# Sixteen-head cross attention on one core: the probabilities of a half-tile step turned and applied in five pieces of 124 instead of twice three of 103

## The chip, the core and the metric

The kernel is one program on one NeuronCore of a Trainium2 chip. The metric is device time in microseconds (us), the median of several executions. The engines named here are TensorE (PE in the rows, with its weight loads as PEld), VectorE (DVE), ScalarE (ACT), GpSimd (POOL) and SyncE (SP), which only issues DMAs.

## The reference, cut to what matters

Four blocks follow each other on x of shape (4, 512, 128). Each is a cross attention and an FFN with several experts. The change touches the first three attentions only, which have 16 heads of width 8 and attend to 77 context rows per batch:

```python
q = split_heads(queries @ Wq + bq)          # b, 16 heads, 512, 8
k = split_heads(keys @ Wk + bk)             # b, 16 heads,  77, 8
v = split_heads(values @ Wv + bv)
scores = jnp.einsum('bhqd,bhkd->bhqk', q, k) / jnp.sqrt(jnp.float32(HD))
scores = jnp.where(mask, jnp.float32(-1e15), scores)
attn = jax.nn.softmax(scores, axis=-1)
ctx = jnp.einsum('bhqk,bhkd->bhqd', attn, v)
x = x + ctx_as_rows @ Wo + bo               # no Wo in the second attention
```

The second and third are alike up to masks and biases. The fourth attention has 8 heads of width 128 and code of its own.

## The kernel before

x has 2048 rows, held as 16 tiles of 128 query rows on the partitions. An attention `l` (0, 1, 2) walks over 32 steps `n`, two to a tile, `t = n // 2`. A step handles 8 of the 16 heads for one tile, as two groups of 4 heads. A group has 4 x 77 = 308 scores per row, so a step has 616. I call a step without any other work in it a plain step.

TensorE runs iteration `n` in this order, written out by hand: `scores(n)` (two matmuls per group, one with the queries and one that adds the mask), the two `turn`s of step n-2, on odd n `turn_out` (the finished tile is transposed), the two `values` of step n-3, on even n `project` (times Wo), and what the plan `APLAN` adds in that iteration. The additions are `q` (the next batch's queries), `v` (`spread_values`, the next batch's value matrix), `x` (transposes of a finished batch for the FFN), and in the first and third attention `l` and `c` (routing). `turn_out` and `project` do not exist in the second attention.

A `turn(k)` transposes one group's 308 probabilities, padded to 309, in three pieces of 103 (line L1925), into PSUM bank 4 or 5. ScalarE copies them to one of four buffers `pT` (L1007, 103 x 384). `values(k)` multiplies the three pieces with three slices of `vx` and accumulates them in a window of 126 columns of bank 6 (L1938). Each fp32 matmul of L1938 shows as two rows in the trace, so a step has 12. `vx` is a value matrix with zeros wherever the head of a row is not the head of a column. It is built for each batch by `spread_values` (L1894, three matmuls, six rows in the trace) and by VectorE's `values_low` (L1409), which multiplies with the mask `cmask`.

VectorE does `shift(n)`: the row maximum of each head (L1422) and the subtraction (L1425). ScalarE follows with the exponential (L1001). VectorE also divides by the sums (`norm`, L1432 and L1437, on odd n), adds to x (L1450), takes statistics (L1456, L1459), and makes the low parts of q (L1273, L1276) and x (L1250).

Scores, `q`, `v`, `x`, `l` and `c` share a ring of two pairs of PSUM banks. An item waits until the item two places ahead of it has been read: scores(n) waits for `shift(n-2)` in a plain stretch, and for VectorE's `values_low` or low part of q if a `v` or `q` stands in that place.

The constants `cmask`, `spread` and the ones in `vx` are made once by GpSimd at the start (L686 to L715). The semaphore `consts` releases TensorE and VectorE after them.

Of the kernel before, what the change touches and what calls it, by code (L numbers as in the profile page):

```python
# [4 lines left out]
B, S, D = 4, 512, 128  # L5
KC = 77
P = 128
# [9 lines left out]
NCH = 3  # L17
CH = -(-GW // NCH)
GWP = NCH * CH
VC = HD + 1  # L20
VW, VSTEP = 126, 6
OSTEP = 128 + HG * VC - VSTEP
# [26 lines left out]
def build(nc, x_in, ctx_t, ctx_rows, mask0, mask1, mask2, attn_w, cols, rows, gates,  # L49
# [8 lines left out]
    with stack:  # L58
# [31 lines left out]
        def ycols(b):  # L90
# [29 lines left out]
        cmask = sb("cmask", [CH, NCH, NG, HG])  # L120
        spreadp = sb("spreadp", [KC, GWP])
        spread = spreadp[:, 0:GW].rearrange("k (h c) -> k h c", h=HG)
# [12 lines left out]
        probs = [shared[:, 2 * NG * GW + s * NG * GWP:2 * NG * GW + (s + 1) * NG * GWP]  # L135
                 .rearrange("p (g k) -> p g k", g=NG) for s in range(2)]
        act_out = [sb(f"act_out{s}", [P, 512]) for s in range(2)]
        pT = [sb(f"pT{s}", [CH, NCH * P])[:, :] for s in range(2)] + [act_out[s][0:CH, 0:NCH * P] for s in range(2)]
# [537 lines left out]
        def _(pool):  # L676
# [26 lines left out]

            for j in range(NCH):
                g.affine_select(out=cmask[:, j], in_=cmask[:, j], compare_op=ALU.is_ge, fill=0.0,
                                base=CH * j, pattern=[[0, NG], [-KC, HG]], channel_multiplier=1)
            st.link(g.affine_select(out=spread, in_=spread, compare_op=ALU.not_equal, fill=1.0, base=0,
                                    pattern=[[0, HG], [-1, KC]], channel_multiplier=1))
            for j in range(NCH):
                g.affine_select(out=cmask[:, j], in_=cmask[:, j], compare_op=ALU.is_ge, fill=0.0,  # L710
                                base=KC - 1 - CH * j, pattern=[[0, NG], [KC, HG]], channel_multiplier=-1)
# [208 lines left out]
        def _(act):  # L920
# [72 lines left out]
            def attention(l):  # L993
                f, lo = FFNS[l], (0 if l == 0 else 1)

                def softmax(n):
                    act.wait_ge(s_used, NSTEP * l + n + 1)
                    if n >= 4:
                        act.wait_ge(pt_ready, 2 * (NSTEP * l + n - 3))
                    t, g = n // 2, slice(2 * (n % 2), 2 * (n % 2) + 2)  # L1000
                    a.activation(probs[t % 2][:, g, 0:GW], shifted[t % 2][:, g, :], ACT.Exp).then_inc(p_ready, 1)  # L1001
# [236 lines left out]
        def _(dve):  # L1238
# [163 lines left out]
            def attention(l):  # L1402
                f, lo = FFNS[l], (0 if l == 0 else 1)

                def values_low(b, o):
                    dve.wait_ge(vx_ps, B * l + b + 1)
                    if b >= 2:
                        dve.wait_ge(pv_done, 2 * NSTEP * l + 16 * (b - 1))
                    v.tensor_tensor(  # L1409
                        vx[b % 2][:, :, :, 0:HD].rearrange("r j h d -> r (j h) d"),  # L1410
                        bank(o)[0:CH, 0:NCH * D].rearrange("r (n d) -> r n d", d=HD),
                        bcast(cmask[:].rearrange("r j g h -> r (j g h)"), HD, 2),
                        ALU.mult).then_inc(vx_ready, 1)
# [14 lines left out]
                def norm(t):  # L1428
                    dve.wait_ge(pv_done, 2 * NSTEP * l + 4 * t + 4)
                    o4 = psum[:, 6 * 512:6 * 512 + NG * OSTEP].rearrange("p (g c) -> p g c", g=NG)[:, :, 0:HG * VC  # L1430
                        ].rearrange("p g (h c) -> p g h c", h=HG)
                    st.link(v.reciprocal(rden[:].rearrange("p (g h) -> p g h", g=NG), o4[:, :, :, HD]))  # L1432
# [4 lines left out]
                    v.tensor_tensor(onorm[t % 2][:].rearrange("p (g h) d -> p g h d", g=NG), o4[:, :, :, 0:HD],  # L1437
                                    bcast(rden[:].rearrange("p (g h) -> p g h", g=NG), HD, 3), ALU.mult
                                    ).then_inc(o_used, 1)
# [30 lines left out]
                for s in range(2):  # L1470
                    st.link(v.memset(probs[s][:, :, GW:GWP], 0.0))
# [284 lines left out]
        def _(pe):  # L1756
# [110 lines left out]
            def attention(l):  # L1867
# [46 lines left out]
                def turn(k):  # L1914
                    n, t, g = k // 2, k // 4, k % 4
# [8 lines left out]
                    for j in range(NCH):  # L1924
                        ins = nc.tensor.transpose(bank(4 + k % 2)[0:CH, j * P:(j + 1) * P],  # L1925
# [3 lines left out]
                def values(k):  # L1929
                    t, g, b = k // 4, k % 4, k // 16  # L1930
                    if k % 16 == 0:
                        pe.wait_ge(vx_ready, B * l + b + 1)
                    if g == 0 and t:
# [3 lines left out]
                    for j in range(NCH):  # L1937
                        ins = mm(bank(6)[:, g * P:g * P + VW], pT[k % 4][:, j * P:(j + 1) * P],  # L1938
# [393 lines left out]
```

## Time and profile before

| | us |
|---|---|
| three runs | 1611.57, 1616.33, 1621.27 |
| median | 1616.33 |
| the profiled execution | 1614.35 |
| its span in the trace | 1612.6 |
| TensorE busy in the span | 1405.3 (87%) |
| VectorE busy | 1096.3 (68%) |
| ScalarE busy | 957.3 (59%) |
| mean granted TensorE clock | 0.951 of full speed |

The three changed attentions lie at about 43 to 160 us, 277 to 380 us and 653 to 764 us of the span. The rest is the four FFNs and the fourth attention. Rows are read like this: start, duration, engine, line, operation, output <- input, partitions x elements. Rows of one kind that follow each other are merged, with their count. In brackets stand the idle time before the row and what ended it.

### The profile page before, as it was taken

The numbers are of one execution on the slowest core, as the hardware profiler recorded it, in microseconds if no ns is written. First come the engines' busy times: TensorE is split into PE (matmuls) and PEld (weight loads), VectorE is DVE, ScalarE is ACT, GpSimd is POOL, SyncE is SP. The second block draws the span as 40 slices with busy tenths as digits, with TensorE's granted clock in tenths as the row PEclk, the third lists the DMA queues.
The fourth block names the chain that finished last, engine by engine and source line by source line (L and its number), as shares of the span: only waits on it lengthen the run. The fifth ranks groups of instructions, "written<-read, shape, count | busy, mean of one in ns | idle before, by whom it ended". The sixth has DMA issues, their size and how long they took to land. (4 is left out here: it accounts for less than half of the span.)

```text
span 1612.6 us, 24666 instructions
## 1 busy us (share of the span) xinstructions
PE 1405.3 (87%) x8205; PEld 1203.9 (75%) x8205; DVE 1096.3 (68%) x2253; ACT 957.3 (59%) x1895; POOL 517.6 (32%) x860
## 2 busy tenths in 40 slices
PE   5799898999999999899899996998898988727773
PEld 5699575898888888798688875887786877527773
DVE  3676689786666667776577775776776766536664
ACT  3456776565555555556777775665565665426661
POOL 5324522303112111422321112222434424355673
PEclk7899999999999999999999998899999999859997
DMA  6111141110000010121121000920000000034542
GB/s 160 54 39 40 45 160 61 40 60 1 4 37 21 20 40 7 35 69 52 40 79 66 26 1 16 190 31 1 6 10 1 14 1 6 9 119 154 158 155 88
DMA packets 57533, 85.22 MB, mean 53 GB/s; under 512 B 9400, under 2 KB 39536, under 8 KB 56127
## 3 DMA queue, kind: packets, MB, share of 16 engines
q1 hardware_dynamic: 54911, 79.40, 18.1%
q0 software_dynamic: 2496, 4.24, 0.8%
q8 instruction: 67, 1.10, 0.3%
q14 instruction: 59, 0.48, 0.1%
HBM read 57.90 MB, written 15.78 MB: 46 GB/s over the span
## 5 line engine op out<-in xcount | busy, mean ns | idle before, releaser
L1553 DVE TENSOR_TENSOR hhl<-psum,hhl 128x512 fp32r<-128x512 f32 x336 | 230.2, 686 | 94.6 <-ACT hhl L1074 92.8
L1760 PE MATMUL psum<-xh,wl 128*128 128x512 f32 (+1 forms) x520 | 203.9, 392 | 7.7 <-DVE logits L1285 4.2
L1761 PE MATMUL psum<-xl,wh 128*128 128x512 f32 (+1 forms) x528 | 202.6, 384 | 0.0
L1762 PE MATMUL psum<-xh,wh 128*128 128x512 f32 (+1 forms) x528 | 202.2, 383 | 0.0
L1074 ACT ACTIVATE hhl<-psum 128x512 fp32r<-128x512 f32 x336 | 199.4, 594 | 0.7 <-DVE psum L1549 0.7
L1146 ACT ACTIVATE hhl<-psum 128x512 fp32r<-128x512 f32 (+1 forms) x160 | 95.3, 596 | 136.9 <-PE psum L2157 136.5
L884 POOL TENSOR_SCALAR shared<-shared,xrd 128x589 f32<-128x589 f32 x128 | 97.7, 765 | 231.4 <-DVE xrd L1647 230.7
L1064 ACT ACTIVATE psum<-psum 128x512 f32<-128x512 f32 x208 | 121.2, 583 | 74.4 <-PE psum L1762 73.3
L1062 ACT ACTIVATE act_out<-psum 128x512 f32<-128x512 f32 x128 | 76.4, 598 | 119.7 <-PE psum L1762 119.3
L1549 DVE TENSOR_TENSOR psum<-act_out,psum 128x512 f32<-128x512 f32 x128 | 88.9, 695 | 84.2 <-PE psum L1762 75.7
L1652 DVE TENSOR_TENSOR hhl<-psum,hhl 128x512 fp32r<-128x512 f32 (+1 forms) x160 | 110.2, 689 | 52.1 <-ACT hhl L1146 51.8
L2060 PE MATMUL psum<-hhl,wl 128*128 128x512 f32 x336 | 135.7, 404 | 10.6 <-DVE hhl L1553 8.7
L2061 PE MATMUL psum<-hhl,wh 128*128 128x512 f32 x336 | 133.0, 396 | 0.0
L2062 PE MATMUL psum<-hhl,wh 128*128 128x512 f32 x336 | 132.4, 394 | 0.0
L801 POOL TENSOR_SCALAR wh<-wraw 128x512 fp32r<-128x512 f32 (+1 forms) x42 | 29.5, 703 | 290.1 <-PE psum L2062 279.9
L1760 PEld LDWEIGHTS psum<-xh,wl 128*128 128x128 f32 x520 | 98.4, 189 | 28.5 <-DVE logits L1285 4.9
L1762 PEld LDWEIGHTS psum<-xh,wh 128*128 128x128 f32 x528 | 100.9, 191 | 21.2
L1761 PEld LDWEIGHTS psum<-xl,wh 128*128 128x128 f32 x528 | 100.7, 191 | 19.0
L1641 DVE TENSOR_REDUCE xnm<-psum 128x1 f32<-128x589 f32 x128 | 97.5, 762 | 21.6 <-PE psum L1762 20.7
L2157 PE MATMUL psum<-ident,shared 128*128 128x128 f32 (+1 forms) x640 | 98.4, 277 | 13.4 <-POOL shared L884 13.3
L1138 ACT ACTIVATE shared<-psum,xnm 128x589 f32<-128x589 f32 x128 | 96.0, 750 | 15.3 <-DVE xnm L1641 14.1
L1422 DVE TENSOR_REDUCE smax<-psum 128x8 f32<-128x616 f32 x96 | 76.2, 794 | 38.3 <-PE psum L1910 38.1
(370 smaller groups left out, 3725.7 us busy)
## 6 DMA issues: line engine op xcount, KB each, us to landing
shared<-in_f_dram SPq DMA_DIRECT2D x16, 768.0 KB
shared<-comb_dram SPq DMA_DIRECT2D x10, 1024.0 KB
xs_dram<-wraw SPq DMA_DIRECT2D x2, 4615.0 KB
shared<-comb_dram SPq DMA_DIRECT2D x24, 256.0 KB, 5.4
wraw<-in_f_dram SPq DMA_DIRECT2D x8, 768.0 KB
xn<-in_f_dram SPq DMA_DIRECT2D x7, 768.0 KB
wraw<-in_f_dram SPq DMA_DIRECT2D x9, 512.0 KB
hhl<-qh SPq DMA_DIRECT2D x64, 64.0 KB, 2.0
```

Of the source, the lines that this page charges most:

```text
L884: g.tensor_scalar(xprob[m % XS], xprob[m % XS], xrd[:, z], 1.0, ALU.mult, ALU.mult).then_inc(x_norm, 1)
L1064: ins = a.activation(h_bank(f, k), h_bank(f, k), f.func)
L1074: a.activation(hh[k % 4], h_bank(f, k), ACT.Copy).then_inc(f.hh_done, 1)
L1553: v.tensor_tensor(hl[k % 4], h_bank(f, k), hh[k % 4].bitcast(f32), ALU.subtract).then_inc(f.h_ready, 1)
L1652: v.tensor_tensor(hl[k % 4][r, :], bank(5 + k % 2)[r, :], hh[k % 4][r, :].bitcast(f32), ALU.subtract).then_inc(xt_lo, 1)
L1760: mm(dst, ll, rh, start=start, stop=False)
L1761: mm(dst, lh, rl, start=False, stop=False)
L1762: return mm(dst, lh, rh, start=False, stop=stop)
L2060: mm(dst, lo[:, o:o + P], hh[k % 4], start=(c == 0), stop=False)
L2061: mm(dst, hi[:, o:o + P], hl[k % 4], start=False, stop=False)
L2062: mm(dst, hi[:, o:o + P], hh[k % 4], start=False, stop=(c == f.nf - 1)).then_inc(f.h_used, 1)
L2157: ins = nc.tensor.transpose(bank(5 + k % 2)[r, qt * P:(qt + 1) * P], xprob[(4 * u + qt) % XS][:, j * P:j * P + r.stop], ident[:])
```

## The change

The two groups of 4 heads of a step become one row of 8 heads with 616 probabilities, padded to 620, in five pieces of 124. The first `turn`, ScalarE copy and `values` of a step take three of the pieces (`PARTS[0]`), the second take two. All five accumulate in one window of 126 columns. `vx` now has five slices instead of three, and `cmask`, `spread` and `spread_values` grow with it. The value matrix of a batch has 5 x 128 = 640 columns in PSUM instead of 384 and lies across two banks of its pair. Two of the four `pT` buffers move into the weight array `aw`, and the exponential writes one contiguous row of 616.

```diff
-NCH = 3
-CH = -(-GW // NCH)
-GWP = NCH * CH
+PH = 2 * HG
+PW = PH * KC
+NCH = 5
+CH = -(-PW // NCH)
+PWP = NCH * CH
+PARTS = (range(0, 3), range(3, NCH))
...
-VW, VSTEP = 126, 6
-OSTEP = 128 + HG * VC - VSTEP
+VW, VSTEP = 126, 18
+OSTEP = 128 + PH * VC - VSTEP
...
-        cmask = sb("cmask", [CH, NCH, NG, HG])
-        spreadp = sb("spreadp", [KC, GWP])
+        cmask = sb("cmask", [CH, NCH, 2, PH])
+        spreadp = sb("spreadp", [KC, PWP])
...
-        pT = [sb(f"pT{s}", [CH, NCH * P])[:, :] for s in range(2)] + [act_out[s][0:CH, 0:NCH * P] for s in range(2)]
+        pT = [aw[0:CH, 4 * P + 3 * P * s:4 * P + 3 * P * (s + 1)] for s in range(2)] + [
+            act_out[s][0:CH, 0:3 * P] for s in range(2)]
...
-                    a.activation(pT[k % 4], bank(4 + k % 2, NCH * P)[0:CH, :], ACT.Copy).then_inc(pt_done, 1)
+                    w = len(PARTS[k % 2]) * P
+                    a.activation(pT[k % 4][:, 0:w], bank(4 + k % 2, w)[0:CH, :], ACT.Copy).then_inc(pt_done, 1)
...
-                        bank(o)[0:CH, 0:NCH * D].rearrange("r (n d) -> r n d", d=HD),
+                        psum[0:CH, o * 512:o * 512 + NCH * D].rearrange("r (n d) -> r n d", d=HD),
...
-                        ins = mm(bank(o)[0:CH, j * D:(j + 1) * D], spreadp[:, j * CH:(j + 1) * CH],
+                        ins = mm(psum[0:CH, o * 512 + j * D:o * 512 + (j + 1) * D], spreadp[:, j * CH:(j + 1) * CH],
...
-                    for j in range(NCH):
-                        ins = nc.tensor.transpose(bank(4 + k % 2)[0:CH, j * P:(j + 1) * P],
+                    for i, j in enumerate(PARTS[k % 2]):
+                        ins = nc.tensor.transpose(bank(4 + k % 2)[0:CH, i * P:(i + 1) * P],
                                                   probs[t % 2][:, g, j * CH:(j + 1) * CH], ident[:])
...
-                    for j in range(NCH):
-                        ins = mm(bank(6)[:, g * P:g * P + VW], pT[k % 4][:, j * P:(j + 1) * P],
+                    for i, j in enumerate(PARTS[k % 2]):
+                        ins = mm(bank(6)[:, g * P:g * P + VW], pT[k % 4][:, i * P:(i + 1) * P],
```

TensorE's instructions of iteration 3 of the first attention (the one with a `spread_values`) before, as the program lists them. L1908 and L1910 are the scores, L1925 the turns, L1938 the values, L1894 the spreading and L1775 an `x` item:

```order
L1908 MATMUL psum<-kb,hhl 128x308
L1910 MATMUL psum<-maskneg,identb 128x308
L1908 MATMUL psum<-kb,hhl 128x308
L1910 MATMUL psum<-maskneg,identb 128x308
L1925 MATMUL psum<-ident,shared 103x128 x6
L1938 MATMUL psum<-vx0,pT0 128x126 x3
L1938 MATMUL psum<-vx0,pT1 128x126 x3
L1894 MATMUL psum<-vrows,spreadp 103x128 x3
L1775 MATMUL psum<-ident,xn 128x128 x4
```

The same iteration now, with line numbers 8 higher:

```order
L1916 MATMUL psum<-kb,hhl 128x308
L1918 MATMUL psum<-maskneg,identb 128x308
L1916 MATMUL psum<-kb,hhl 128x308
L1918 MATMUL psum<-maskneg,identb 128x308
L1933 MATMUL psum<-ident,shared 124x128 x5
L1946 MATMUL psum<-vx0,aw 128x126 x5
L1902 MATMUL psum<-vrows,spreadp 124x128 x5
L1783 MATMUL psum<-ident,xn 128x128 x4
```

Nothing changes its place. The turns and the values have one instruction less each, the spreading has two more.

VectorE at the end of its iteration 4 of the first attention before (the step's maximum and subtraction, then the value matrix, then work on the gate weights):

```order
L1250 TENSOR_TENSOR xl<-psum,xh 128x512
L1422 TENSOR_REDUCE smax<-psum 128x8
L1425 TENSOR_TENSOR shared<-psum,smax 128x616
L1409 TENSOR_TENSOR vx<-psum,cmask 103x48x8
L1535 TENSOR_SCALAR gwg<-gw,pcols 128x8
```

And now:

```order
L1258 TENSOR_TENSOR xl<-psum,xh 128x512
L1430 TENSOR_REDUCE smax<-psum 128x8
L1433 TENSOR_TENSOR shared<-psum,smax 128x616
L1417 TENSOR_TENSOR vx<-psum,cmask 124x80x8
L1543 TENSOR_SCALAR gwg<-gw,pcols 128x8
```

The place is the same, and the value matrix has 80 x 8 elements per row instead of 48 x 8.

## Rows read from the trace of the kernel before

**Rows 1.** The page: its span.

```profile
span 1612.6 us, 24666 instructions
```

**Rows 2.** Busy time by stretch: TensorE, weight loads, VectorE, ScalarE, GpSimd, clock, DMA.

```profile
120.00:140.00 20.00, 20.00 (x173) 18.94 (x173) 15.44 (x38) 13.17 (x30) 7.37 (x26) 1.00 0.17 51
300.00:320.00 20.00, 19.42 (x161) 17.81 (x160) 16.41 (x38) 11.03 (x22) 2.61 (x10) 1.00 0.13 31
353.00:368.00 15.00, 15.00 (x130) 14.12 (x129) 13.40 (x32) 9.79 (x19) 2.60 (x10) 1.00 0.01 1
```

**Rows 3.** Timeline, a plain step of the second attention on TensorE.

```profile
305.85 0.39 PE L1908 MATMUL psum<-kb,hhl 96*128 96x308 f32 x1
...
306.53 0.82 PE L1925 MATMUL psum<-ident,shared 128*103 128x128 f32 x6
...
307.18 1.50 PE L1938 MATMUL psum<-vx,pT 103*128 103x126 f32 x12
...
308.44 0.47 PE L1760 MATMUL psum<-xh,wql 128*128 128x512 f32 x1
```

**Rows 4.** Timeline, four transposes of full width and what follows them.

```profile
329.07 0.60 PE L1775 MATMUL psum<-ident,xn 128*128 128x128 f32 x4
329.43 0.39 PE L1908 MATMUL psum<-kb,k 96*128 96x308 f32 x1
```

**Rows 5.** Timeline, one `spread_values` and the item behind it.

```profile
290.85 0.82 PE L1894 MATMUL psum<-vrows,spreadp 77*103 77x128 f32 x6
291.50 0.60 PE L1775 MATMUL psum<-ident,xn 128*128 128x128 f32 x4
```

**Rows 6.** Groups by line and form over the span: count, busy us, mean ns, idle before.

```profile
L1409 DVE TENSOR_TENSOR vx<-psum,cmask 103x384 f32<-103x384 f32 x12 | 6.6, 549 | 1.4 <-PE psum L1894 1.3
...
L1425 DVE TENSOR_TENSOR shared<-psum,smax 128x616 f32<-128x616 f32 x96 | 76.7, 799 | 3.3
```

**Rows 7.** Timeline, iterations 10 and 12 of the second attention: what releases the next scores.

```profile
309.22 0.30 PE L1908 MATMUL psum<-kb,hhl 96*128 96x308 f32 x1
...
311.56 0.74 DVE L1273 SCALAR_TENSOR_TENSOR ql<-psum,pcols,qh 128x512 fp32r<-128x512 f32 x1
...
312.35 0.41 PE L1908 MATMUL psum<-kb,hhl 96*128 96x308 f32 x1 [0.39 <-DVE ql L1273]
...
315.61 0.39 PE L1908 MATMUL psum<-kb,hhl 96*128 96x308 f32 x1
...
318.04 0.55 DVE L1409 TENSOR_TENSOR vx<-psum,cmask 103x384 f32<-103x384 f32 x1
...
318.64 0.41 PE L1908 MATMUL psum<-kb,hhl 96*128 96x308 f32 x1 [0.19 <-DVE vx L1409]
```

**Rows 8.** Timeline, VectorE over one tile of the second attention (two plain steps).

```profile
300.98 0.26 DVE L1432 RECIPROCAL rden<-psum 128x16 f32<-128x16 f32 x1 [0.36 <-PE psum L1938]
...
304.14 0.80 DVE L1422 TENSOR_REDUCE smax<-psum 128x8 f32<-128x616 f32 x1 [0.25 <-PE psum L1910]
...
306.13 0.26 DVE L1432 RECIPROCAL rden<-psum 128x16 f32<-128x16 f32 x1 [0.36 <-PE psum L1938]
```

**Rows 9.** Timeline, first attention, from the stall at 64 us to the one at 77.

```profile
64.56 0.30 PE L1946 MATMUL psum<-ident,onorm 128*128 128x128 f32 x1 [2.37 <-DVE onorm L1437]
...
64.69 2.64 PE L1938 MATMUL psum<-vx,pT 103*128 103x126 f32 x12
...
70.65 0.47 PE L1997 MATMUL psum<-ident,wraw 77*128 77x77 f32 x4
...
71.58 0.51 SPq L569 DMA_DIRECT2D hhl<-qh  x1
```

**Rows 10.** Timeline, the start: GpSimd's last constant and VectorE's first instruction.

```profile
6.62 0.43 POOL L715 COPY vx<-cmask 103x48 f32<-103x48 f32 x2
...
8.17 0.54 DVE L1369 TENSOR_SCALAR wraw<-psum,pcols 128x308 f32<-128x308 f32 x1 [8.17 <-DMA bo<-in_rows_dram]
...
12.10 0.87 DVE L1354 BATCH_NORM_STATS2 stats<-x 128x6 f32<-128x128 f32 x4 [1.57 <-DMA x<-in_x_dram]
```

More of the change, by code:

```diff
@@ L119, in build @@
         hm32 = sb("hm32", [KS, HG])
-        cmask = sb("cmask", [CH, NCH, NG, HG])
-        spreadp = sb("spreadp", [KC, GWP])
-        spread = spreadp[:, 0:GW].rearrange("k (h c) -> k h c", h=HG)
+        cmask = sb("cmask", [CH, NCH, 2, PH])
+        spreadp = sb("spreadp", [KC, PWP])
+        spread = spreadp[:, 0:PW].rearrange("k (h c) -> k h c", h=PH)
         kb = sb("kb", [P, 10 * S], f32r)
@@ L134, in build @@
                    for s in range(2)]
-        probs = [shared[:, 2 * NG * GW + s * NG * GWP:2 * NG * GW + (s + 1) * NG * GWP]
-                 .rearrange("p (g k) -> p g k", g=NG) for s in range(2)]
+        probs = [shared[:, 2 * NG * GW + s * 2 * PWP:2 * NG * GW + (s + 1) * 2 * PWP]
+                 .rearrange("p (g k) -> p g k", g=2) for s in range(2)]
         act_out = [sb(f"act_out{s}", [P, 512]) for s in range(2)]
-        pT = [sb(f"pT{s}", [CH, NCH * P])[:, :] for s in range(2)] + [act_out[s][0:CH, 0:NCH * P] for s in range(2)]
+        pT = [aw[0:CH, 4 * P + 3 * P * s:4 * P + 3 * P * (s + 1)] for s in range(2)] + [
+            act_out[s][0:CH, 0:3 * P] for s in range(2)]
         oT = [act_out[s][:, 384:512] for s in range(2)]
@@ L999, in softmax @@
                         act.wait_ge(pt_ready, 2 * (NSTEP * l + n - 3))
-                    t, g = n // 2, slice(2 * (n % 2), 2 * (n % 2) + 2)
-                    a.activation(probs[t % 2][:, g, 0:GW], shifted[t % 2][:, g, :], ACT.Exp).then_inc(p_ready, 1)
+                    t, g = n // 2, n % 2
+                    a.activation(probs[t % 2][:, g, 0:PW],
+                                 shifted[t % 2][:, 2 * g:2 * g + 2, :].rearrange("p g k -> p (g k)"),
+                                 ACT.Exp).then_inc(p_ready, 1)
                 def copy_pT(k):
@@ L1429, in norm @@
                     dve.wait_ge(pv_done, 2 * NSTEP * l + 4 * t + 4)
-                    o4 = psum[:, 6 * 512:6 * 512 + NG * OSTEP].rearrange("p (g c) -> p g c", g=NG)[:, :, 0:HG * VC
-                        ].rearrange("p g (h c) -> p g h c", h=HG)
-                    st.link(v.reciprocal(rden[:].rearrange("p (g h) -> p g h", g=NG), o4[:, :, :, HD]))
+                    o4 = psum[:, 6 * 512:6 * 512 + 2 * OSTEP].rearrange("p (g c) -> p g c", g=2)[:, :, 0:PH * VC
+                        ].rearrange("p g (h c) -> p g h c", h=PH)
+                    st.link(v.reciprocal(rden[:].rearrange("p (g h) -> p g h", g=2), o4[:, :, :, HD]))
                     if l == 1:
@@ L1914, in turn @@
                 def turn(k):
-                    n, t, g = k // 2, k // 4, k % 4
+                    n, t, g = k // 2, k // 4, k // 2 % 2
                     if k % 2 == 0:
@@ L1929, in values @@
                 def values(k):
-                    t, g, b = k // 4, k % 4, k // 16
+                    t, g, b = k // 4, k // 2 % 2, k // 16
                     if k % 16 == 0:
                         pe.wait_ge(vx_ready, B * l + b + 1)
-                    if g == 0 and t:
+                    if k % 4 == 0 and t:
                         pe.wait_ge(o_used, NT * l + t)
```

12 lines of the change are left out of this document (6 added, 6 removed).

## The prediction, made before the changed kernel was run

> **What bounds the kernel now.** I first read the page for the span and the clock, then the busy time by stretch inside the three attentions, then the timeline of single steps on TensorE and VectorE. The changed code runs in about 330 of the 1612.6 us [rows 1]. There TensorE is the bound: 20.00 of 20 us busy at 120 to 140, 19.42 at 300 to 320, 15.00 of 15 at 353 to 368, all at a granted clock of 1.00 (2.4 GHz) [rows 2]. VectorE comes second: 13.40 of those last 15 us. ScalarE has room with 9.79. So an instruction taken from TensorE is worth its time only until VectorE's chain is met, and the question is how often that happens.
>
> **The removed work.** A plain step of the second attention takes 308.44 - 305.85 = 2.59 us [rows 3]: 0.68 for scores, 0.65 for the six turns (0.108 each), 1.26 for the twelve value rows (0.105 each). The change takes away one turn and one value matmul, which is two rows: 0.108 + 0.210 = 0.318 us per step, 96 steps, 30.5 us at most. The pieces are larger, 124 instead of 103. For a transpose that is a wider weight tile. Transposes of 128 columns follow each other at (329.43 - 329.07) / 4 = 0.09 us [rows 4], no slower than those of 103, so I take the price per instruction as unchanged. For the values only the rows of the contraction grow, and I take the 126-column price as it is. The second ScalarE copy of a step shrinks from 384 to 256 columns; ScalarE is not waited for, so that is worth nothing.
>
> **The added work.** `spread_values` goes from three matmuls to five, six rows to ten. Six take 291.50 - 290.85 = 0.65 us [rows 5], so four more cost 0.43 us, twelve times: 5.2 us on TensorE. VectorE's value matrix goes from 384 to 640 elements. The nearest rows are 549 ns at 384 elements and 799 ns at 616, both fp32 products of PSUM and SBUF [rows 6]: 250 ns for 232 elements, so 640 elements come to about 0.82 us, +0.28. From below that could be +0 if the length did not count, from above 549 x 640 / 384 = 915 ns, +0.37. I take the slope of the two rows. GpSimd's constants at the start grow (four more selects, twice the width of `spread`), an estimate of 1 to 2 us. They end at 7.05 us, VectorE waits for a DMA until 8.17 and again 1.57 us for x before 12.10 [rows 10]; I cost it at nothing, and at up to 1 us if that cover is gone.
>
> **Where the removed time arrives.** I sort the iterations by what ends them.
>
> (a) TensorE is full, no item of the ring stands in the way. I count 18 such steps in the first attention, 23 in the second, 22 in the third: iterations 5 to 8 (not in the first attention), 9, 13 to 17 and 21 to 33, without 27 in the first and third. 63 x 0.318 = 20.0 us gained, and three last values outside, 0.6. Sum -20.7.
>
> (b) The iteration after a `q` is ended by VectorE's low part of q: scores at 309.22, low part done at 312.30, next scores at 312.35 [rows 7]. This chain begins at the scores and has nothing of the change in it. Iterations 10 and 18 everywhere, and 27 in the first and third attention, where routing stands in that place: eight steps, 0.
>
> (c) Iterations with a spreading (3, 11, 19). TensorE has 0.43 more and 0.32 less: +0.12, six times, 0.7. In three of them (3 in the first attention, 19 in the first and third) the spreading itself waits for VectorE, so only the +0.43 counts: 1.3. Sum +2.0.
>
> (d) The iteration after the spreading (4, 12, 20) is ended by the value matrix on VectorE: scores at 315.61, value matrix 318.04 + 0.55, next scores at 318.64 [rows 7]. It gets longer by 0.28, nine times, and once more at the start of the third attention, where VectorE is late: +2.8. Here the change costs directly what it was meant to save elsewhere.
>
> (e) The first attention's stretch from 64.5 to 71 us. SyncE's queue reloads wraw there and waits for the transposes of 70.65 that read it; the query DMAs of the next batch go out behind it at 71.58 and TensorE stands until they land [rows 9]. Between lie twelve value rows at half clock (2.64 us, about 0.20 a row), one turn block and one more value block at full clock. 0.40 + 0.11 + 0.21 = 0.7 us gained. Before 64.5 us VectorE is the bound, so the steps there gain nothing.
>
> (f) In the second attention both engines come to about the same length. From 300.98 to 306.13 VectorE has 5.15 us for two steps, of which it waits 0.25 and 0.36 [rows 8]; so it needs some 4.54. TensorE would need 2 x 2.27 = 4.54. A tie between two engines that wait for each other costs something: I put 0.035 us on each of 14 steps, +0.5.
>
> Sum: -20.7 + 2.0 + 2.8 - 0.7 + 0.5 = -16.1 us. From the profiled execution, 1612.6 of span and 1.75 around it, that gives 1598.2. That execution was 2.0 us under the median of the three runs; from the median it gives 1600.2. I forecast 1600.
>
> **A rule against it.** The trace shows transposes of 128 columns in 0.09 us each and of 103 in 0.108 [rows 3, 4], so width does not show in their spacing. The Trainium skill, "TensorE: Matmul & The Clock Gate", section "LDWEIGHTS (loading the stationary operand)", says that a weight load takes time in proportion to its columns and not to the rows of the contraction. By that rule, if loads set the pace, five wide turns would take as long as six narrow ones. The trace does not agree with it as the bound here; that result is the third rival.
>
> **The rivals.**
>
> 1. The full TensorE gain. VectorE's chains of (b) and (d) give way because VectorE is less pressed elsewhere. Then 30.5 - 5.2 = 25.3 us arrive: 1591. For it: VectorE is busy only 15.44 of 20 us in the first attention [rows 2]. Against it: those chains start at the scores, not at VectorE's backlog [rows 7]. 10%.
>
> 2. VectorE becomes the bound. Already 13.40 of 15 us in the second attention [rows 2]; with the larger value matrix, and TensorE no longer slower, the steps stop at VectorE's pace everywhere. Then about half of (a) arrives, 10.3 less: 1600.2 + 10.3 = 1610.5. Against it: in the first and third attention a plain step has a transpose and a projection more on TensorE and VectorE has several tenths free. 16%.
>
> 3. The turns cost by their width. Five at 0.108 x 124 / 103 = 0.130 take 0.65, as six do now. Then 63 x 0.108 = 6.8 us of (a) are lost: 1607. Against it: rows 4. 7%.
>
> 4. Slower than before, by the clock. TensorE is full now at 1.00 in these stretches. If it stands often enough for the granted clock to fall to 1.2 GHz there, a step costs much more: the value rows take 2.64 instead of 1.50 us [rows 3, 9], 1.14 more, and turns and scores about as much again, some 2.4 us a step as an estimate. Seven such steps undo the gain, ten more than that cost 24: with twelve in all the time is 1600 + 29 = 1629. For it: every attention now has more waits. Against it: 300 to 320 has 0.58 us of idle time and a clock of 1.00 [rows 2], and the new waits are tenths of a microsecond. 5%.
>
> **How the numbers follow.** My forecast 62%, the rivals 10, 16, 7 and 5. The chip's own spread, 1611.57 to 1621.27 in three runs, is as wide as half the effect, and where the clock dips in the later stages may shift with the start of the FFNs by a few microseconds either way. The range takes in rival 1 with 2 us below and rival 2: 1589 to 1611. Left out are rival 4 and the tails. 0.5% is 8 us, about what a measurement of this kernel can tell from no change: the bound is 1608.3. Faster: 0.62 x 0.96 + 0.10 + half of rival 3 and a fifth of rival 2, 0.77. Slower by over 0.5% is rival 4, 0.05. Same: 0.18.
>
> **What would show it.** The plain step of the second attention should fall from 2.59 to between 2.27 and 2.32 us, and that of the first and third, which is longer by a transpose or a projection, by 0.32. Turns and value rows keep 0.108 and 0.105 us apart. The value matrix takes 0.82 us, and the wait of scores for it grows. Iterations 12 and 20 get longer by 0.28, iteration 10 stays at 3.13. The FFNs and everything behind 766 us keep their lengths. I am wrong if plain steps fall by less than 0.25 (VectorE in front), if the turns' spacing rises (width), or if the clock inside an attention falls below 1.00 where it was 1.00 before.

## The result and the profile after

| | us |
|---|---|
| before, 19 runs | 1614.69 (1607.76 to 1621.27) |
| after, 19 runs | 1603.85 (1598.80 to 1610.52) |
| ratio | 0.9933, 95% interval 0.9920 to 0.9945 |
| profiled execution after, its span | 1601.09, 1599.4 |

The change takes 10.8 us off, an interval of 9 to 13. The forecast was 16.1. The profiled executions are 13.2 us apart in span, so about 2 of those are the spread between executions.

The page after, for [rows 1]: 476 instructions fewer on all engines together.

```profile
span 1599.4 us, 24190 instructions
```

Busy time by stretch (TensorE, weight loads, VectorE, ScalarE, GpSimd, clock, DMA), for [rows 2], and then the three attentions as windows from their first scores to the scores of their last step. First the kernel after:

```profile
300.00:320.00 20.00, 18.48 (x151) 16.81 (x150) 17.42 (x38) 11.94 (x26) 2.60 (x10) 1.00 0.17 41
43.58:145.69 102.11, 90.09 (x671) 80.83 (x670) 78.34 (x177) 53.48 (x121) 32.95 (x79) 0.92 0.16 43
272.64:358.04 85.40, 76.85 (x607) 68.86 (x606) 74.34 (x159) 53.58 (x112) 21.88 (x54) 0.98 0.17 47
643.25:737.28 94.03, 83.96 (x667) 75.97 (x665) 72.01 (x157) 56.43 (x128) 31.59 (x71) 0.98 0.15 43
```

The same three windows of the kernel before:

```profile
45.49:149.41 103.92, 93.97 (x744) 85.47 (x743) 78.33 (x179) 56.77 (x122) 33.47 (x80) 0.97 0.16 42
278.10:368.52 90.42, 85.70 (x679) 78.19 (x678) 73.52 (x158) 56.87 (x113) 21.60 (x53) 0.95 0.16 45
654.56:750.91 96.35, 91.12 (x739) 83.79 (x738) 71.67 (x158) 59.82 (x129) 32.12 (x74) 0.98 0.16 42
```

Over the three windows TensorE is busy 19.9 us less (270.8 to 250.9), but they last only 9.2 us less (290.7 to 281.5). The other 10.7 us are new idle time of TensorE. In the second attention it is 8.9 us less work and 5.0 us less time. VectorE works 1.2 us more (223.5 to 224.7).

A plain step of the second attention on TensorE, for [rows 3]:

```profile
296.54 0.39 PE L1916 MATMUL psum<-kb,hhl 96*128 96x308 f32 x1
...
297.22 0.71 PE L1933 MATMUL psum<-ident,shared 128*124 128x128 f32 x5
297.76 1.28 PE L1946 MATMUL psum<-vx,act_out 124*128 124x126 f32 x10
298.80 0.39 PE L1916 MATMUL psum<-kb,hhl 96*128 96x308 f32 x1
```

It takes 2.26 us: 0.68 for scores, 0.54 for five turns, 1.04 for ten value rows. Before it was 2.59.

Iterations 10 to 12 of the same attention, on TensorE and VectorE, for [rows 7]:

```profile
301.90 0.31 PE L1916 MATMUL psum<-kb,hhl 96*128 96x308 f32 x1
...
304.24 0.74 DVE L1281 SCALAR_TENSOR_TENSOR ql<-psum,pcols,qh 128x512 fp32r<-128x512 f32 x1
...
305.04 0.41 PE L1916 MATMUL psum<-kb,hhl 96*128 96x308 f32 x1 [0.72 <-DVE ql L1281]
...
307.39 1.26 PE L1902 MATMUL psum<-vrows,spreadp 77*124 77x128 f32 x10
308.40 0.38 PE L1916 MATMUL psum<-kb,hhl 96*128 96x308 f32 x1
...
310.82 0.81 DVE L1417 TENSOR_TENSOR vx<-psum,cmask 124x640 f32<-124x640 f32 x1
...
311.69 0.41 PE L1916 MATMUL psum<-kb,hhl 96*128 96x308 f32 x1 [0.80 <-DVE vx L1417]
```

Iteration 10 lasts 3.14 us as before, and the wait inside it has grown from 0.39 to 0.72: the 0.33 us taken from TensorE became a wait. Iteration 12 lasts 3.29 instead of 3.03, with a wait of 0.80 where there was 0.19.

### The profile page after: what moved, and what is told of

Same layout as the page of the kernel before. It is cut to its first block and busy times, and to the rows that moved or that the text cites. A ratio compares the mean times of both kernels' runs of the same rounds, so it can differ in the third digit from the quotient of the medians.

```text
span 1599.4 us, 24190 instructions
## 1 busy us (share of the span) xinstructions
PE 1381.8 (86%) x7965; PEld 1177.0 (74%) x7965; DVE 1098.4 (69%) x2253; ACT 947.2 (59%) x1895; POOL 519.3 (32%) x864
## 5 line engine op out<-in xcount | busy, mean ns | idle before, releaser
L2165 PE MATMUL psum<-ident,shared 128*128 128x128 f32 (+1 forms) x640 | 98.6, 277 | 13.3 <-POOL shared L889 13.2
```

What stands on the lines that cost most here:

```text
L2165: ins = nc.tensor.transpose(bank(5 + k % 2)[r, qt * P:(qt + 1) * P], xprob[(4 * u + qt) % XS][:, j * P:j * P + r.stop], ident[:])
```

## How the experiments are read

The time of a whole run moves by several us between executions of one program, which is most of what is to be told apart here. What lies outside the three windows is 1313 to 1324 us in all 14 profiles, whatever the edit. So I give for each run the median, the ratio to the kernel before on the same chip, and the windows. A window comes from one profiled execution.

The windows are not all equally steady. Two profiles of the kernel after agree within 0.1 us in each, but two profiles of one reordered kernel (e3_vq_first and e3_again) differ by 0.5, 0.9 and 0.8 us in the three, with both signs, and only their sums, 270.40 and 270.03, lie close together. The differences lie in iterations 0 to 9, where TensorE leaves waits of 1 to 4 us and the granted clock is at half in places. The last column holds iterations 10 to 30 of the three attentions alone. There the granted clock is 1.00 in every profile, and the two pairs of profiles agree within 0.05 us. It is the firmest number here.

| kernel | median | ratio (95%) | windows 1, 2, 3 | sum | iterations 10 to 30 |
|---|---|---|---|---|---|
| before | 1614.69 | 1 | 103.92, 90.42, 96.35 | 290.69 | 189.24 |
| after | 1603.85 | 0.9933 (0.9920 to 0.9945) | 102.11, 85.40, 94.03 | 281.54 | 180.47 |
| after_again | 1603.85 | 0.9929 (0.9908 to 0.9949) | 102.18, 85.35, 94.00 | 281.53 | 180.42 |
| e1_small_vx | 1599.74 | 0.9894 (0.9875 to 0.9913) | 99.00, 83.95, 92.21 | 275.16 | 176.34 |
| e7_before_big_vx | 1620.36 | 1.0034 (1.0018 to 1.0050) | 108.96, 92.51, 102.30 | 303.77 | 193.33 |
| e5_extra_turn | 1609.10 | 0.9961 (0.9946 to 0.9976) | 103.51, 88.36, 96.14 | 288.01 | 183.93 |
| e6_extra_value | 1618.73 | 1.0022 (1.0008 to 1.0037) | 107.02, 90.53, 98.72 | 296.27 | 189.38 |
| e2_v_first | 1597.45 | 0.9880 (0.9861 to 0.9900) | 100.76, 84.58, 92.27 | 277.61 | 175.61 |
| e3_vq_first | 1593.91 | 0.9854 (0.9832 to 0.9876) | 100.13, 81.30, 88.97 | 270.40 | 172.86 |
| e3_again | 1595.11 | 0.9869 (0.9843 to 0.9895) | 99.67, 82.21, 88.15 | 270.03 | 172.85 |
| e8_gate_later | 1586.40 | 0.9828 (0.9801 to 0.9856) | 93.28, 81.75, 88.99 | 264.02 | 172.78 |
| e9_logits_first | 1580.61 | 0.9788 (0.9758 to 0.9817) | 91.68, 81.60, 86.81 | 260.09 | 169.99 |
| e4_before_vq_first | 1608.19 | 0.9925 (0.9902 to 0.9948) | 105.07, 87.06, 92.92 | 285.05 | 185.13 |
| e10_before_all | 1597.04 | 0.9879 (0.9855 to 0.9902) | 97.30, 87.44, 93.99 | 278.73 | 183.62 |

The theory is that of the prediction: TensorE's steps get shorter by what is removed, except where VectorE's low part of q or its value matrix ends them, and the larger value matrix costs its full length there.

## Is the larger value matrix on the path? e1 and e7

e1 spreads and masks three slices of `vx` instead of five; it leaves out slices 3 and 4 of every value matrix, which stay zero.

```diff
-                    for j in range(NCH):
+                    for j in range(3):
                         ins = mm(psum[0:CH, o * 512
...
-                        vx[b % 2][:, :, :, 0:HD]
+                        vx[b % 2][:, 0:3, :, 0:HD]
```

> The changed kernel, but the value matrix is built as small as before: three spreading matmuls instead of five, and VectorE multiplies 384 columns instead of 640 (slices 3 and 4 keep zeros, so that part of the values is left out). Theory (the added work sits on the path): nine spreading steps lose 0.43 us on TensorE each, ten waits for the value matrix lose 0.28 us each, so 3.9 + 2.8 = 6.7 us less than the changed kernel: a ratio to before near 0.989. Rival (the added work is hidden beside other work and the missing gain lies elsewhere): no more than 2 us less, ratio 0.992 to 0.993.

The windows fall by 6.4 us, the ratio by 0.0039. VectorE's product on the path, in e1:

```profile
304.90 0.55 DVE L1419 TENSOR_TENSOR vx<-psum,cmask 124x384 f32<-124x384 f32 x1
...
305.50 0.41 PE L1918 MATMUL psum<-kb,hhl 96*128 96x308 f32 x1 [0.53 <-DVE vx L1419]
```

Iteration 11 of the second attention goes from 3.36 to 2.93 (0.43), iteration 12 from 3.29 to 3.02 (0.27), iteration 4 from 3.92 to 3.66 (0.26). Over all nine pairs of such iterations the spreading gives 3.9 us and the value matrix 2.3, and iterations 10 to 30, which hold six of the pairs, fall by 4.1. Both terms of the prediction arrive in full, with nothing hidden. That the windows' 6.4 is so near the 6.2 is in part chance: iteration 6 of the first attention is 1.3 us shorter as well, and iterations 0 to 2 of the second and third are 0.9 longer together.

e7 does the reverse on the kernel before: it spreads and masks 640 columns, of which 384 are used.

```diff
-                        bank(o)[0:CH, 0:NCH * D]
+                        psum[0:CH, o * 512:o * 512 + 5 * D]
...
-                    for j in range(NCH):
+                    for j in range(5):
+                        c = min(j, 2) * CH
```

> The kernel before with the larger value matrix alone: five spreading matmuls and 640 columns on VectorE, of which the values read three slices as before (two of the pT buffers lie in the weight array, as in the changed kernel, for want of room). Theory: 3.9 us on TensorE and 2.5 to 2.8 us of waits, 6.5 us slower than before, ratio 1.004. Rival (the longer value matrix costs only because TensorE got faster): 4 us, ratio 1.0025.

The medians give +5.3 us, between the two expectations. The second attention's window gives +2.1, which is 3 x (0.43 + 0.27). Iterations 10 to 30 give +4.1, which is 6 x (0.43 + 0.27). The first and third windows give +5.0 and +6.0, of which some 2 each lie at the changed items. The rest lies elsewhere: iteration 3 of the third attention lasts 7.93 instead of 3.69 us, iterations 6 and 8 of the first 5.06 and 5.33 instead of 3.93 and 4.10. These are places where TensorE comes out of a long wait (the granted clock is 0.50 from 668 to 680 us in e7), and the section on the prediction returns to them. The windows' sum of +13.1 is that of one execution, 4.4 us slower than e7's median, and it lies outside what the ratio allows (3 to 8 us).

## What is one turn worth, and one value matmul? e5 and e6

e5 adds to the kernel after one transpose per step, of a piece that is turned anyway, into columns that nobody reads.

```diff
+                    if k % 2:
+                        ins = nc.tensor.transpose(bank(4 + k % 2)[0:CH, 2 * P:3 * P],
+                                                  probs[t % 2][:, g, 4 * CH:5 * CH], ident[:])
                     ins.then_inc(pt_ready, 1)
```

> The changed kernel with a sixth transpose in each step (the last piece once more, into columns that nobody reads). Theory: only in the steps that TensorE fills does it cost, about 60 of 96 by 0.108 us: 6.5 us more than the changed kernel (10.4 if every step paid; 0 if VectorE were the bound). Rival (a turn of 124 columns is dearer than one of 103): 0.130 us each, 8 us or more, and the spacing of the turns in the trace is 0.13.

It is 5.2 us behind after_again by the medians, 6.5 by the windows and 3.5 in iterations 10 to 30. Its plain step, after five turns:

```profile
303.58 0.71 PE L1933 MATMUL psum<-ident,shared 128*124 128x128 f32 x5
304.12 0.27 PE L1936 MATMUL psum<-ident,shared 128*124 128x128 f32 x1
304.23 1.28 PE L1949 MATMUL psum<-vx,act_out 124*128 124x126 f32 x10
```

Five wide turns take 0.54 us and the sixth 0.11. They cost by the piece and not by their width. The rule of the Trainium skill ("TensorE: Matmul & The Clock Gate", section "LDWEIGHTS (loading the stationary operand)") that the time of a weight load goes by its columns does not set the pace here: loads of 124 columns and of 103 both leave transposes 0.108 us apart.

The windows' 6.5 equals the expectation by chance, since iteration 3 of the second attention is 1.7 us longer at a granted clock of 0.69. In iterations 10 to 30 the 43 steps of (a) that lie there would give 43 x 0.108 = 4.6 us, and 3.5 arrive. Iterations 23 of the first and third attention and 27 and 29 of the second even get shorter, by 0.11 to 0.23 us, with one transpose more. In these TensorE was not the bound.

e6 adds one value matmul per step to the kernel after; one piece is accumulated twice, so the output differs.

```diff
+                    if k % 2:
+                        ins = mm(bank(6)[:, g * P:g * P + VW], pT[k % 4][:, P:2 * P], ...)
                     ins.then_inc(pv_done, 1)
```

> The changed kernel with a sixth value matmul in each step (a piece accumulated twice, so the output differs). Theory: 60 steps by two rows of 0.105 us, 12.6 us more than the changed kernel. If VectorE had become the bound of most steps, less than 5. In the second attention, where VectorE needs about 2.27 us a step, the plain step goes from 2.28 to 2.48.

It is 14.9 us behind after_again by the medians and 14.7 by the windows, where 12.6 was expected, and 9.0 in iterations 10 to 30, which is 43 x 0.21. The rest lies in iterations 0 to 9. A plain step of the second attention goes from 2.24 to 2.47 or 2.48. TensorE is the bound there: more work shows at once.

Together the two prices are 0.11 + 0.23 = 0.34 per plain step, close to the 0.32 to 0.34 that the change took away.

## Does VectorE's order of work decide the rest? e2, e3, e4

In an iteration VectorE does the row maximum and the subtraction of the newest scores first (1.54 us) and the value matrix or the low part of q after them. e2 puts the value matrix ahead, e3 both, e4 is e3's edit on the kernel before. The edit of e3:

```diff
                         if what == "x":
                             x_low(f.index, b, bank(ring_bank(l, ("x", b))))
+                        elif what == "q":
+                            q_low(l, b, bank(ring_bank(l, ("q", b))))
+                        elif what == "v":
+                            values_low(b, ring_bank(l, ("v", b)))
                     if n < NSTEP:
                         shift(n)
...
-                        if what == "q":
-                            q_low(l, b, bank(ring_bank(l, ("q", b))))
-                        elif what == "v":
-                            values_low(b, ring_bank(l, ("v", b)))
-                        elif what == "l":
+                        if what == "l":
```

> The changed kernel with one move: VectorE makes the value matrix before the maximum and subtraction of its iteration instead of after them. Theory (iterations 4, 12 and 20 of each attention are ended by the chain scores, maximum, subtraction, value matrix): those nine steps fall from about 3.3 to about 2.5 us where TensorE can fill them, some 0.7 us each, 6 us in all: ratio to before near 0.9895. Rival (VectorE as a whole is the bound, so order does not matter): within 1.5 us of the changed kernel, ratio 0.993.

> As the last one, and the low part of q too is made before the maximum of its iteration. Theory: iterations 10 and 18 as well fall from 3.13 to about 2.5 to 2.6 us, six steps by some 0.55 us, 3 us more than the last kernel and 9 to 10 less than the changed one: ratio near 0.9875. Rival (VectorE's whole work is the bound): as the changed kernel.

> The kernel before with the same two moves. Theory: there the steps with these chains are only 0.2 to 0.4 us longer than TensorE needs, so the moves give 3 to 4.5 us: ratio 0.997 to 0.998. If they give as much as on the changed kernel (9 us), the chains cost the same before and the change did not run into them.

e3 makes the windows 11.1 us shorter than after, and in a second comparison 11.5; in iterations 10 to 30 it is 7.6 both times. In the second attention iterations 10, 12, 18 and 20 fall from 3.14, 3.29, 3.23 and 3.28 to 2.18, 2.26, 2.27 and 2.24: they are now full on TensorE. Part comes back in the iteration behind. Iterations 11 and 19 rise from 3.36 to 4.10 and 3.83. The rows of e3_again there:

```profile
301.00 0.75 DVE L1281 SCALAR_TENSOR_TENSOR ql<-psum,pcols,qh 128x512 fp32r<-128x512 f32 x1 [0.81 <-ACT qh L949]
...
304.15 1.35 PE L1946 MATMUL psum<-vx,aw 124*128 124x126 f32 x10 [0.52 <-issue]
```

VectorE now stands 0.81 us for ScalarE's high part of q ahead of the row maximum, the exponential and the copies are late by that, and TensorE waits for them one iteration later.

e2 alone is worth 3.9 us in the windows, 4.9 in iterations 10 to 30 and 8.6 by the ratios (0.0053), with 6 expected; the ratios are uncertain by some 4 us. In the second attention it takes 3.6 us from iterations 4, 12 and 20, but iteration 3 rises from 3.80 to 5.46, and iteration 5 from 2.27 to 3.44, where TensorE waits 0.91 us for the divided tile. For iteration 3 the clock column of e2 shows why (the last but two), just behind a wait of 1.36 us for `ql` that after has too, with 1.32:

```profile
281.00:284.00 3.00, 2.87 (x12) 2.53 (x13) 1.43 (x3) 2.08 (x5) 2.84 (x3) 0.50 0.27 66
284.00:287.00 3.00, 3.00 (x26) 2.94 (x24) 0.24 (x1) 0.19 (x2) 2.92 (x3) 0.89 0.44 107
```

e4 gave more than expected: 0.9925 where 0.997 to 0.998 was written. Its windows are 5.6 us shorter than before's and iterations 10 to 30 are 4.1 shorter, close to the expected 3 to 4.5; the ratio says 12 with an interval of 8 to 16. What the difference between the two is, these runs don't tell.

## Two more of VectorE's places, and the change's price there: e8, e9, e10

In the first attention VectorE makes the routing's gate weights (seven small operations) before it divides the first finished tile. In e3_again:

```profile
59.19 1.07 DVE L1543 TENSOR_SCALAR gwg<-gw,pcols 128x8 f32<-128x8 f32 x1
...
62.56 0.29 DVE L1549 TENSOR_SCALAR betaB<-betaB,pcols 128x128 f32<-128x128 f32 x1
62.77 0.25 DVE L1440 RECIPROCAL rden<-psum 128x16 f32<-128x16 f32 x1
...
63.49 0.45 PE L1954 MATMUL psum<-ident,onorm 128*128 128x128 f32 x1 [4.31 <-DVE onorm L1445]
```

e8 is e3 with that piece one iteration later. e9 is e8 with VectorE's read of the routing logits ahead of the row maximum.

```diff
-                    if l == 0 and n == 4:
+                    if l == 0 and n == 5:
```

```diff
                         elif what == "v":
                             values_low(b, ring_bank(l, ("v", b)))
+                        elif what == "l":
+                            read_logits(f, b, bank(ring_bank(l, ("l", b))))
...
-                            take_logits(f, b, bank(ring_bank(l, ("l", b))))
+                            use_logits(f, b)
```

> The same kernel as e3_vq_first, so that the next two can be compared on one chip. Both theories: about 1594 to 1596 us, 0.985 to 0.987 of the kernel before.

> e3 with the first attention's gate weights given to VectorE one iteration later. In e3 the first attention's step 5 takes 8.11 us, with 4.32 us in which TensorE waits for VectorE's norm (onorm) before the finished tile can be transposed. Theory: VectorE's order of work is what TensorE waits for there, so moving the piece gives back part of the 4.3 us, 2 to 4 us in all, 0.001 to 0.0025 less than e3's ratio. Rival: the gate weights are only put off and stop the next step instead, or the wait is for data and not for order; then the ratio is that of e3.

> e8 with VectorE's read of the routing logits put ahead of the iteration's row maximum; the rest of the routing work stays behind it. In the trace of after TensorE waits about 0.47 us for that read in iterations such as 19 and 28 of the first and third attention. Theory: four such waits go, about 2 us less than e8 (0.001 of the ratio). Rival: the row maximum is then late by the same time, ScalarE and the next turns with it, and nothing is gained.

e8 is worth 6.4 us in the first attention's window (6.85 against the profile of e3_vq_first) and 0.0041 of the ratio (6.6 us, uncertain by more than half of it). That is more than the stall itself, and more than the 2 to 4 us expected. The wait is 0.72 now:

```profile
58.42 0.25 DVE L1440 RECIPROCAL rden<-psum 128x16 f32<-128x16 f32 x1
...
59.14 0.30 PE L1954 MATMUL psum<-ident,onorm 128*128 128x128 f32 x1 [0.72 <-DVE onorm L1445]
```

Iteration 5 falls from 7.96 to 3.50 us (-4.5). Iterations 6 and 7 fall by another 1.8, and the stretch at half clock behind the stall is gone. (In e3_vq_first, the same program as e3_again, iteration 6 took 3.99 us and not 4.81, and iterations 8 and 9 took 4.69 and 3.70 and not 4.11 and 3.18: the time at half clock came later.) The four us behind it in e3_again, and the same place in e8:

```profile
64.00:68.00 4.00, 4.00 (x19) 3.66 (x19) 1.65 (x3) 1.12 (x3) 0.00 (x0) 0.50 0.00 0
```

```profile
60.00:64.00 4.00, 3.70 (x34) 3.39 (x33) 3.77 (x10) 1.56 (x4) 1.33 (x2) 1.00 0.02 4
```

For e9 four waits of 0.47 were expected to go, about 2 us; the windows fall by 3.9 and the ratio by 0.0040 (6.5 us, uncertain by more than half of it). Iterations 19 and 27 of the first and third attention fall by 0.70 to 0.72 each, 2.9 together. The column of waits had put these too low: it counts from the modelled end of the last matmul. Ten value rows take 1.04 us in the plain step until the next row starts, so TensorE was free from 127.22 + 1.04 = 128.26 and stood 0.70 us until 128.96. In iterations 10 to 30 the gain is 2.8. Iteration 3 of the third attention gives 0.7 more, but it also differs by 0.8 between the two profiles of e3's kernel. In e8 and then in e9:

```profile
127.22 1.28 PE L1946 MATMUL psum<-vx,aw 124*128 124x126 f32 x10
...
128.51 0.17 DVE L1292 COPY logits<-psum 128x32 f32<-128x32 f32 x1
128.72 0.19 DVE L1293 TENSOR_TENSOR logits<-logits,psum 128x32 f32<-128x32 f32 x1
...
128.96 0.41 PE L1916 MATMUL psum<-kb,hhl 96*128 96x308 f32 x1 [0.47 <-DVE logits L1293]
```

```profile
127.34 0.19 DVE L1296 COPY logits<-psum 128x32 f32<-128x32 f32 x1
...
127.57 0.19 DVE L1297 TENSOR_TENSOR logits<-logits,psum 128x32 f32<-128x32 f32 x1
...
129.46 0.39 PE L1926 MATMUL psum<-kb,hhl 96*128 96x308 f32 x1
```

e9, with 1580.61 us, beats both kernels. e10 has the same three edits of VectorE's order on the kernel before.

> The kernel before with e9's three edits of VectorE's order and without the change; beside e9 (0.9788 of the kernel before, 1580.61 us) it prices the change where fewer of VectorE's waits stand in its way. Theory: in e4 and e3, with only the first of the three edits, the change was worth 14.3 us; with steps 19 and 27 and the first attention's step 5 freed as well it should be worth 15 to 18 us, so this kernel comes to 0.988 to 0.990. Rival: the change gives 10.8 us whatever the order; then 0.9855. Bound from above: 25.3 us, 0.9945.

| VectorE's order | windows without the change | with it | the change is worth | in iterations 10 to 30 | by the ratios |
|---|---|---|---|---|---|
| as it was | 290.69 | 281.54 | 9.2 | 8.8 | 10.8 |
| value matrix and low part of q first | 285.05 | 270.2 | 14.8 | 12.3 | 9 to 11.5 |
| all three edits | 278.73 | 260.09 | 18.6 | 13.6 | 14.7 |
| an estimate without any waits | | | 23.2 | 17.5 | |

The last row is 87 x 0.108 + 84 x 0.210 - 9 x 0.43, since the windows hold the turns of 87 steps and the values of 84; for iterations 10 to 30 it is 63 x 0.318 - 6 x 0.43. Iterations 10 to 30, at full clock in every profile, show that the change's worth grows by half, from 8.8 to 13.6 us, as VectorE's waits are taken away. The windows alone would say that it doubles, but 5.0 of the 18.6 us lie in iterations 0 to 9, and 1.7 of these in iteration 3 of the third attention (5.49 us in e10, 3.79 in e9), whose length differs from one profile of a program to the next. The ratios go the same way at the ends, but each of them is uncertain by 2 to 4 us, so they alone would not show it.

## The prediction, step by step

**The direction, and most steps, were right; the size was 16.1 where 10.8 was measured.** Inside the three windows the prediction's terms make -12.9 us: 54 of the 63 steps of (a) lie there (-17.2), (c) +2.0, nine of (d) +2.5, (e) -0.7, (f) +0.5. Measured are -9.2. By attention: forecast -3.7, -4.7, -4.5, measured -1.8, -5.0, -2.3. The first and third are each 2 us short. The second looks right, but 0.7 of its 5.0 us come from iterations 0 to 2, for which nothing was forecast. Iterations 10 to 30 of all three were to give -10.2 and gave -8.8; iterations 0 to 9 were to give -2.7 and gave -0.4. Behind the windows nine steps and three last values were to give 3.5 us, and the profile shows 2.4 from the scores of iteration 31 to the last value matmul.

**The closeness of 1600 to 1603.85 is in part luck.** The gain was forecast 5.3 us too large. The forecast started from 1616.33, the median of three runs, and that of 19 is 1614.69, which hid 1.6 of it. (A slip without weight: the chance of faster adds up to 0.76 and not to 0.77.)

**The removed work: right.** Turns keep 0.108, value rows 0.104, the plain step 2.26 lies under the 2.27 that was the lower end [rows 3]. 50 of the 54 steps of (a) got shorter by 0.20 to 0.35.

**The added work: right.** Ten spreading rows take 1.09 or 1.01 us instead of 0.65 [rows 5], and the value matrix 817 ns where 0.82 was taken from the slope of two rows [rows 6]:

```profile
L1417 DVE TENSOR_TENSOR vx<-psum,cmask 124x640 f32<-124x640 f32 x12 | 9.8, 817 | 1.1 <-PE psum L1902 1.0
```

GpSimd's constants end 1.15 us later [rows 10], and VectorE's first instruction starts 0.24 later, so the cover held:

```profile
7.69 0.51 POOL L720 COPY vx<-cmask 124x80 f32<-124x80 f32 x2
```

```profile
8.41 0.54 DVE L1377 TENSOR_SCALAR wraw<-psum,pcols 128x308 f32<-128x308 f32 x1 [8.41 <-POOL vx L720]
```

**(b) right for five of eight.** Iteration 10 stays within 0.01 in all three attentions, 27 too. Iteration 18 is 0.1 longer in all three. In e6, whose steps are longer by a value matmul, it takes 4.08, 3.18 and 4.01 us, against 4.08, 3.13 and 4.01 before. So it depends on how fast TensorE came to it, and not only on a chain that begins at its scores, as the prediction had it. What makes the 0.1 was not traced.

**(c) and (d) right.** Iteration 11 got longer by 0.10 or 0.11, iteration 19 by 0.45, 0.10 and 0.45, iterations 12 and 20 by 0.26 or 0.27, iteration 4 by 0.18, 0.26 and 0.27. e1 shows that these are the larger value matrix and nothing else.

**(f) about right.** In the second attention iterations 27 and 29 gained nothing of 0.32 (+0.08 and -0.06), 7, 15 and 23 lost 0.07 of it each and 17 lost 0.12. That is 1.0 us where 0.5 was put, in few steps rather than in all. VectorE as the bound everywhere, the second rival, is out: in 18 of 20 steps the removed work arrived, and e6 shows TensorE's work on the path.

**What failed, first: step (a) counted too many.** It took iterations 23 and 31 of the first and third attention for full on TensorE. In after, iteration 23 is 0.1 us longer, not 0.32 shorter:

```profile
123.22 0.20 DVE L1313 TENSOR_TENSOR comb<-m2w,rank 128x32 f32<-128x32 f32 x1
...
124.48 0.29 DVE L1445 TENSOR_TENSOR onorm<-psum,rden 128x128 f32<-128x128 f32 x1
...
124.92 0.30 PE L1954 MATMUL psum<-ident,onorm 128*128 128x128 f32 x1 [0.26 <-DVE onorm L1445]
```

VectorE has the routing's four `comb` operations and an update of x ahead of the division there, and TensorE needs the divided tile. Before, TensorE had no wait at this place, but little to spare: the divided tile was ready at 126.33 us and TensorE took it at 126.52. VectorE still stood 0.45 us ahead of the row maximum of iteration 22; after, the rows show no idle time of VectorE from there to the division, and the two steps ahead are 0.33 us shorter each. That e5 makes iteration 23 shorter again, 3.18 us instead of 3.31, fits a VectorE that is late. Two such steps inside the windows cost 0.9 us of the forecast, and the two iterations 31, where TensorE waits 0.25 and 0.26 us for the same tile, as much behind them. The check that was left out: for each kind of iteration, how long VectorE's chain to the next thing that TensorE needs is and how much idle time VectorE has ahead of it, not only whether TensorE was idle before.

**Second: step (e), and the start of the third attention.** At several places where TensorE leaves a long wait its granted clock is at half, and these stretches lie elsewhere after than before. The first attention after, behind the stall of 2.43 us [rows 9]:

```profile
63.46 2.35 PE L1946 MATMUL psum<-vx,aw 124*128 124x126 f32 x10
```

```profile
60.00:64.00 4.00, 1.57 (x11) 1.36 (x11) 3.76 (x10) 1.04 (x3) 1.80 (x2) 0.81 0.00 0
64.00:68.00 4.00, 4.00 (x20) 3.66 (x20) 1.64 (x3) 1.15 (x3) 0.00 (x0) 0.50 0.00 0
```

Before, the stretch from 66 to 70 us, behind the same stall, had 0.70. Iteration 6 lasts 4.77 us there instead of 3.93 (4.85 in the second profile). With iteration 5, which is 0.24 shorter, step (e) comes to +0.6 instead of -0.7. In the third attention iteration 3 lasts 5.42 instead of 3.69 (5.41 in the second profile). Before:

```profile
661.44 1.24 PE L1925 MATMUL psum<-ident,shared 128*103 128x128 f32 x6
...
664.15 0.41 PE L1908 MATMUL psum<-kb,k 96*128 96x308 f32 x1 [1.48 <-DVE ql L1276]
```

After:

```profile
649.44 0.71 PE L1933 MATMUL psum<-ident,shared 128*124 128x128 f32 x5
...
652.84 0.52 PE L1916 MATMUL psum<-kb,k 96*128 96x308 f32 x1 [2.69 <-DVE ql L1284]
```

```profile
652.50:657.20 4.70, 4.36 (x23) 4.01 (x24) 1.89 (x3) 1.62 (x4) 4.45 (x7) 0.64 0.30 73
```

Before, TensorE ran its work of this place at half clock, stood 1.48 us for the same `ql`, and went on at full clock. After, it did that work at full clock, stood 2.69 us, and went on at 0.64. The sum of iterations 2 and 3 rose by 1.9 us. So the fourth rival's mechanism shows, in two places and not in twelve steps, and the prediction's own sign of it (a clock below 1.00 inside an attention where it was 1.00) came true there. Its sum had half clock only in the twelve value rows of (e), and no term for a stretch that moves.

That the change is what moved these stretches is not shown. The kernel before has one profile. In the other kernels without the change iteration 6 of the first attention takes 5.06 (e7), 4.60 (e4) and 3.87 us (e10), and iteration 3 of the third 7.93, 3.70 and 5.49; in kernels with it they take 3.51 to 4.85 and 3.79 to 5.66. Two profiles of e3's kernel differ by 0.8 us at both places (3.99 and 4.81, 4.60 and 3.80). So at these places a forecast to 1 us could not be had from one trace, with or without the change.

The account by stretch: in iterations 10 to 30 the forecast was 1.4 us too good, of which 0.9 are the two iterations 23, 0.3 iteration 18 and 0.5 the steps of (f) beyond its term, with some tenths of the other sign. In iterations 0 to 9 it was 2.3 too good: 1.3 at step (e), 1.8 at iterations 2 and 3 of the third attention (where 0.1 was forecast), less the 0.7 at the start of the second, with tenths elsewhere. The first part repeats within 0.05 us in a second profile of the kernel after; the second lies where the clock stands at half in places.

**The rivals.** First (all of TensorE's gain): out for the kernel after, and e10 to e9 shows what it would take. Third (width): out, by e5. The clock of the fourth: above.

## What to carry to other kernels

Work taken from the engine that is the bound is worth its time only in the iterations that this engine ends. Count them one kind at a time, and for each write down the length of the other engine's chain up to what the bound engine needs next; an iteration with a tenth or two of slack counts as ended by that chain. A change that shortens the bound engine's steps and a change in the other engine's order are worth more together than apart (8.8 and 4.1 us alone, 16.4 together, in iterations 10 to 30), so a small operation that somebody waits for goes ahead of a long one that nobody waits for yet. Behind the long waits of this kernel (1.3 to 4.3 us) an iteration took up to 4 us more or less from one variant to the next, by where the clock stood at half; compare variants over stretches whose granted clock is 1.00 in all of them.

## What the runs showed that was not expected

- The same iteration, with nearly the same wait ahead of it (1.32 and 1.36 us for `ql`), ran at a granted clock of 1.00 in after and of 0.50 in e2, and took 3.80 and 5.46 us. Taking 4.3 us of stall out of the first attention (e8) gave back another 1.8 us behind it against e3_again, where iteration 6 was at half clock.
- A small operation of VectorE can take as long as the one of GpSimd beside it. The `gpad` subtraction of 8 columns took 1.24 us in after, while GpSimd's `wl` of 1.26 ran:

```profile
60.67 1.24 DVE L1546 TENSOR_TENSOR gpad<-gwg,gpad 128x8 fp32r<-128x8 f32 x1
```

```profile
60.63 1.26 POOL L808 TENSOR_TENSOR wl<-wraw,wh 128x512 fp32r<-128x512 f32 x1
```

  In e8, where the last `wl` had ended at 61.42, it took 0.17:

```profile
61.76 0.17 DVE L1546 TENSOR_TENSOR gpad<-gwg,gpad 128x8 fp32r<-128x8 f32 x1
```

  The Trainium skill, "SBUF — State Buffer", section "SBUF: two separate sides", says that an operation of VectorE with two inputs in SBUF and one of GpSimd that reads SBUF lock each other out for a whole instruction. These rows agree with it: they end at 61.91 and 61.89 us. The two operations of VectorE ahead of it, with one tensor in SBUF each, also end 0.03 us behind one of GpSimd (59.97 behind 59.94, 60.57 behind 60.54). It is a part of the first attention's stall that none of my terms had.
- Five value pairs whose left operand lies in `aw` are sometimes followed after 1.11 to 1.13 us and not after 1.04; those from `act_out` take 1.03 or 1.04 in the second attention where scores follow. That is 0.08 us in a few steps of each attention; why was not tried.
- Iterations 10 to 30 of the three attentions repeat within 0.05 us between two executions (180.47 and 180.42 after, 172.86 and 172.85 in e3's kernel), while the whole spans moved by 4.5 and 6.4 us. For a change in one stage such a stretch is the better measure, as long as the clock is the same in it.
